# New slot tables for the last ticks with a scan, and another order of projections and loads in the first ones

## The reference

```python
k = rope(x @ Wk.T)                      # 16 heads of 32
v = x @ Wv.T
W = eye(32) per batch and head
for each block of 16 tokens:            # 256 blocks, strictly in order
    z = kc @ W
    W = W - kc.T @ ((z - vc) * 2 / (16 * 32))
out = layernorm(z over all heads) * gamma + beta
x1 = layernorm(x + out @ Wo.T)
h = silu(x1 @ gate.T * gs) * (x1 @ up.T * us)        # 1408 wide
y = layernorm(x1 + (h @ down.T) * ds)
```

## Time and profile before

| | |
|---|---|
| median of three runs | 1948.31 us |
| the profiled execution | 1948.8 us |
| its span | 1946.7 us |
| TensorE busy | 1856.2 us, 95% |
| VectorE, GpSimd, ScalarE busy | 61%, 33%, 28% |
| DMA | 288.29 MB, mean 148 GB/s |
| mean granted TensorE clock | 0.982 |

### The profile page before, as it was taken

How to read it: one execution, slowest core, us unless ns; L and a number is a source line. 1 busy time by engine, 2 the same in 40 slices (tenths; PEclk the granted TensorE clock), 3 DMA queues, 4 the chain that set the end, 5 groups by cost and what they waited for, 6 DMA issues and landing times.

```text
span 1946.7 us, 60662 instructions
## 1 busy us (share of the span) xinstructions
PE 1856.2 (95%) x25784; PEld 1482.0 (76%) x25784; DVE 1185.3 (61%) x2602; ACT 550.7 (28%) x1238; POOL 652.1 (33%) x783
## 2 busy tenths in 40 slices
PE   7868999999999999999999999999999999888897
PEld 5647787787778778877877777777777777767776
DVE  3655666666666566666666666666666665555543
ACT  3212323232222223222232223233322322222222
POOL 2222333333333333333333333333333333323333
PEclk9978999999999999999999999999999999999999
DMA  8974444554544554554455454445545544443310
GB/s 282 289 225 136 149 138 144 168 155 142 157 147 135 148 163 143 159 149 132 143 161 165 134 155 148 137 145 166 159 141 154 151 126 135 124 123 110 101 61 23
DMA packets 310783, 288.29 MB, mean 148 GB/s; under 512 B 43376, under 2 KB 261616, under 8 KB 310512
## 3 DMA queue, kind: packets, MB, share of 16 engines
q1 hardware_dynamic: 297840, 266.57, 45.9%
q10 hardware_dynamic: 12672, 17.83, 2.8%
HBM read 153.17 MB, written 139.72 MB: 150 GB/s over the span
## 4 chain that ended last, share of the span: by engine, by line
PE 80%; DVE 10%; DMA 4%; SPq 2%; ACT 2%; issue 1%; ACTq 0%; POOL 0%; POOLq 0%; DVEq 0%
PE gu_acc L973 32%; PE work L954 25%; PE down_acc L987 13%; PE scan_acc L926 4%; PE scan_acc L943 4%; DVE x_tok L1153 2%; DMA landed<-x1T_scr 2%; DVE state L1233 2%; DVE hid L1238 2%; DVE turned L1158 2%; SPq L327 1%; ACT hid L689 1%; PE scan_acc L973 1%; SPq L372 1%; PE down_acc L954 1%
## 5 line engine op out<-in xcount | busy, mean ns | idle before, releaser
L579 POOL TENSOR_TENSOR hid_lo<-hid,hid_hi 128x256 fp32r<-128x256 f32 x352 | 262.6, 746 | 644.3 <-ACT hid_hi L699 644.2
L973 PE MATMUL gu_acc<-x_hi,gw 128*128 128x256 f32 x1372 | 379.5, 309 | 11.4 <-DVE hid L1238 5.8
L689 ACT ACTIVATE hid<-gu_acc,gate_scale 128x256 f32<-128x256 f32 x343 | 162.7, 474 | 780.8 <-PE gu_acc L973 780.5
L1238 DVE SCALAR_TENSOR_TENSOR hid<-gu_acc,up_scale,hid 128x256 f32<-128x256 f32 x343 | 165.6, 483 | 317.6 <-ACT hid L689 317.4
L973 PE MATMUL gu_acc<-x_lo,gw 128*128 128x256 f32 x1372 | 343.5, 283 | 0.0
L973 PE MATMUL gu_acc<-x_hi,uw 128*128 128x256 f32 x1372 | 341.4, 281 | 0.0
L973 PE MATMUL gu_acc<-x_lo,uw 128*128 128x256 f32 x1372 | 340.4, 281 | 0.0
L1233 DVE SCALAR_TENSOR_TENSOR state<-scan_acc,half_step,state 128x256 f32<-128x256 f32 x512 | 223.3, 477 | 165.9 <-PE scan_acc L943 161.2
L973 PEld LDWEIGHTS gu_acc<-x_hi,gw 128*128 128x128 f32 x1372 | 261.1, 190 | 48.2 <-DVE hid L1238 21.8
L987 PE MATMUL down_acc<-dw,hid_hi 128*128 128x512 f32 x704 | 282.3, 401 | 2.3 <-POOL hid_lo L579 2.2
L987 PE MATMUL down_acc<-dw,hid_lo 128*128 128x512 f32 x704 | 279.1, 396 | 0.0
(11 more groups left out here) (129 smaller groups left out, 2251.6 us busy)
## 6 DMA issues: line engine op xcount, KB each, us to landing
x_fm<-xT SPq DMA_DIRECT2D x64, 256.0 KB, 3.5
k_rows<-k_scr SPq DMA_DIRECT2D x512, 32.0 KB, 2.0
z_scr<-v_rows SPq DMA_DIRECT2D x32, 512.0 KB, 3.2
z_tok<-z_scr SPq DMA_DIRECT2D x512, 32.0 KB, 1.8
x_tok<-x SPq DMA_DIRECT2D x32, 512.0 KB, 5.7
v_rows<-v_scr SPq DMA_DIRECT2D x496, 32.0 KB, 2.0
out<-x_tok SPq DMA_DIRECT2D x31, 512.0 KB, 2.8
kT_scr<-turned SPq DMA_DIRECT2D x120, 128.0 KB, 2.9
```

The lines of the kernel that those rows point to most:

```text
L579: pool.tensor_tensor(hid_lo[m % RING][:], hid[m % 2], hid_hi[m % RING][:].bitcast(F32), ALU.subtract).then_inc(hid_lo_ready, 1)
L689: act.activation(hid[m % 2], gu_bank(n, m)[:, 0:TOK], ACT.Silu, scale=gate_scale[:, m:m + 1]).then_inc(silu_done, 1)
L973: mm = pe.matmul(gu_bank(n, m)[:, k * TOK:(k + 1) * TOK], lhsT=w[:, c, m * P:(m + 1) * P].bitcast(dt), rhs=part[:, c].bitcast(dt), start=( ...
L1238: dve.scalar_tensor_tensor(hid[m % 2], gu_bank(n, m)[:, TOK:2 * TOK], up_scale[:, m:m + 1], hid[m % 2], ALU.mult, ALU.mult).then_inc(hid_r ...
```

## The change

There are three parts.

1. Ticks 29 to 32 count as late. Tick 29 (TURNING) and ticks 30 to 32 (LATE) get tables of their own, and tick 33 (WITHOUT_SCAN) takes the two blocks of its oldest tile that were done in the tick before. In late ticks all 11 blocks of a tile are in its own tick, 0 to 7 in slots 0 to 7 and 8 to 10 in slots 10 to 12; O is in slots 8 and 9; the z statistics are in slot 1, `turn_zn` in slot 3, the parts of z in slot 7, the norm of x1 in slot 11, `high_x1` and `low_x1` in slot 15.
2. ScalarE's queue loads x of tiles 3 to 6. SyncE's order in ticks 1 and 2 changes with it, and z of tile 0 is loaded in one go in tick 2. Six of the weight pieces are issued later, and all examinations but one or two move back.
3. K and V of tile 3 leave slots 12 to 15 of tick 1 and stand with K and V of tile 4 between slot 15 of tick 1 and tick 2.

```diff
-USUAL, WITHOUT_SCAN, END = None, NT + 1, NT + 2
+STEADY = 3
+LEAD = 3
+USUAL, TURNING, LATE, WITHOUT_SCAN, END = None, NT - LEAD, NT - LEAD + 1, NT + 1, NT + 2
 GATE_UP = {USUAL: {14: (2, 0), 15: (2, 1), 0: (3, 2), 2: (3, 3), 3: (3, 4), 5: (3, 5), 7: (3, 6), 8: (3, 7), 9: (3, 8),
                    10: (3, 9), 11: (3, 10)},
-           WITHOUT_SCAN: {0: (3, 2), 1: (3, 3), 2: (3, 4), 3: (3, 5), 4: (3, 6), 5: (3, 7), 6: (3, 8), 8: (3, 9),
-                          9: (3, 10), 11: (2, 0), 12: (2, 1), 13: (2, 2), 14: (2, 3), 15: (2, 4)},
+           TURNING: {0: (3, 2), 1: (3, 3), 2: (3, 4), 3: (3, 5), 4: (3, 6), 5: (3, 7), 6: (3, 8), 7: (3, 9), 10: (3, 10)},
+           LATE: {0: (3, 0), 1: (3, 1), 2: (3, 2), 3: (3, 3), 4: (3, 4), 5: (3, 5), 6: (3, 6), 7: (3, 7), 10: (3, 8),
+                  11: (3, 9), 12: (3, 10)},
+           WITHOUT_SCAN: {0: (3, 0), 1: (3, 1), 2: (3, 2), 3: (3, 3), 4: (3, 4), 5: (3, 5), 6: (3, 6), 7: (3, 7), 8: (3, 8),
+                          9: (3, 9), 10: (3, 10), 11: (2, 0), 12: (2, 1), 13: (2, 2), 14: (2, 3), 15: (2, 4)},
...
 DOWN = {USUAL: {15: (2, 0), 0: (3, 1), 2: (3, 2), 3: (3, 3), 5: (3, 4), 8: (3, 5), 9: (3, 6), 10: (3, 7), 11: (3, 8),
                 12: (3, 9), 13: (3, 10)},
+        TURNING: {0: (3, 1), 1: (3, 2), 2: (3, 3), 3: (3, 4), 4: (3, 5), 5: (3, 6), 6: (3, 7), 7: (3, 8), 8: (3, 9),
+                  11: (3, 10)},
+        LATE: {1: (3, 0), 2: (3, 1), 3: (3, 2), 4: (3, 3), 5: (3, 4), 6: (3, 5), 7: (3, 6), 8: (3, 7), 11: (3, 8),
+               12: (3, 9), 13: (3, 10)},
...
+       TURNING: DOWN[TURNING], LATE: DOWN[LATE], WITHOUT_SCAN: DOWN[WITHOUT_SCAN], END: DOWN[END]}
-WEIGHED = {(1, 5): (0,), (1, 8): (1,), (1, 11): (2,), (1, 13): (3,), (2, 0): (4,), (2, 2): (5,), (2, 4): (6,), (2, 6): (7,),
-           (2, 9): (8,), (2, 10): (9,), (2, 11): (10,), (2, 13): (11,)}
+WEIGHED = {(1, 6): (0,), (1, 10): (1,), (1, 13): (2,), (2, 0): (3,), (2, 2): (4,), (2, 4): (5,), (2, 6): (6,), (2, 9): (7,),
+           (2, 10): (8,), (2, 11): (9,), (2, 12): (10,), (2, 13): (11,)}
-FIRST_UNITS = ((K, 1, 1), (V, 1, 1), (K, 2, 0), (V, 2, 0), (K, 2, 1), (V, 2, 1), (K, 3, 0), (V, 3, 0))
-MIDDLE_UNITS = ((K, 3, 1), (V, 3, 1), (K, 4, 0), (V, 4, 0))
+FIRST_UNITS = ((K, 1, 1), (V, 1, 1), (K, 2, 0), (V, 2, 0), (K, 2, 1), (V, 2, 1))
+MIDDLE_UNITS = ((K, 3, 0), (V, 3, 0), (K, 3, 1), (V, 3, 1), (K, 4, 0), (V, 4, 0))
+def late(t):
+    return NT - LEAD <= t <= NT
```

On SyncE:

```diff
                     store_v(1, 1)
-                    load_x_fm(3)
+                    load_k_half0(1)
                     store_z(0, 0, NS // 2)
-                    load_k_half0(1)
-                    load_z(0, 0, NS // 2, 16)
                     store_v(2, 0)
+                    store_k(2)
+                    store_v(2, 1)
                     load_v_half0(1, 0)
                     load_v_half0(1, 1)
-                    store_k(2)
                     store_z(0, NS // 2, NS - 1)
-                    store_v(2, 1)
-                    load_x_fm(4)
-                    load_z(0, NS // 2, NS - 1, 32)
                     store_kT(2)
                     store_z(0, NS - 1, NS)
-                    load_z(0, NS - 1, NS, 48)
                 elif t == 2:
                     load_k_half1(1)
                     load_v_half1(1)
                     store_v(3, 0)
+                    load_z(0, 0, NS, 48)
                     store_k(3)
                     store_v(3, 1)
-                    load_x_fm(5)
...
                     load_kT(2)
-                    load_x_fm(6)
                     load_x(0)
```

On ScalarE (the copies and loads of weights besides):

```diff
+                    if t == 1 and s == 7:
+                        load_x_fm(3)
+                    if t == 1 and s == 11:
                         high_x(3, 0)
                     if t == 1 and s == 13:
                         high_x(3, 1)
                     if t == 1 and s == 15:
+                        load_x_fm(4)
                         copy_v(3, 0)
                         high_x(4, 0)
                         copy_v(3, 1)
                         high_x(4, 1)
+                        load_x_fm(5)
                     if t == 2 and s == 1:
                         high_x(5, 0)
+                    if t == 2 and s == 4:
+                        load_x_fm(6)
...
+                    if t == 1 and s in (0, 4, 8, 12):
+                        load_ffn(0, s // 4)
+                    if t == 1 and s in (2, 6, 10, 14):
+                        copy_ffn(1, s // 4)
+                    if t == 1 and s == 15:
                         load_ffn(1, 0)
+                        copy_ffn(2, 0)
+                    if t == 2 and s == 0:
                         load_ffn(1, 1)
                         copy_ffn(2, 1)
+                    if t == 2 and s == 1:
                         load_ffn(1, 2)
+                    if t == 2 and s == 2:
                         copy_ffn(2, 2)
+                    if t == 2 and s == 3:
                         load_ffn(1, 3)
+                    if t == 2 and s == 4:
                         copy_ffn(2, 3)
+                    if t == 2 and s in (5, 6, 7, 8):
+                        load_ffn(2, s - 5)
```

On TensorE (VectorE, ScalarE and GpSimd follow in the same way):

```diff
-                    if within(o) and s in (6, 7):
-                        project_o(o, s - 6)
+                    if within(o) and s in ((8, 9) if late(t) else (6, 7)):
+                        project_o(o, s % 2)
```

More of the change, by code:

```diff
@@ L67, in within @@
     return 0 <= n < NT
+def late(t):
+    return NT - LEAD <= t <= NT
 def unit_at(table, t, s):
-    age, m = table.get(t, table[USUAL]).get(s, (0, -1))
+    age, m = table.get(LATE if late(t) and t != TURNING else t, table[USUAL]).get(s, (0, -1))
     return (t - age, m) if m >= 0 and within(t - age) else None
@@ L627, in tick @@
                         copy_k_cols(t, 0)
-                    if within(o) and s == 9:
+                    if within(o) and s == (11 if late(t) else 9):
                         inverse_root(1, o)
@@ L631, in tick @@
                         low_hid(*unit_at(LOW, t, s))
-                    if within(o) and s == (3 if o == 0 else 4 if o == LAST else 1):
+                    if within(o) and s == (3 if o == 0 else 4 if o == LAST else 2 if late(t) else 1):
                         inverse_root(0, o)
@@ L637, in tick @@
                         add_rotated(n, 1)
-                    if within(o) and s == 4:
+                    if within(o) and s == (7 if late(t) else 4):
                         add_bias(o, 0)
@@ L802, in tick @@
                         high_hid(*unit_at(LOW, t, s))
-                    if within(o) and s == (6 if o == LAST else 5):
+                    if within(o) and s == (6 if o == LAST else 7 if late(t) else 5):
                         high_zn(o, 0)
@@ L812, in tick @@
                         save_z(sc, s // 2)
-                    if within(o) and s == (6 if o in (0, LAST) else 5):
+                    if within(o) and s == (6 if o in (0, LAST) else 7 if late(t) else 5):
                         high_zn(o, 1)
@@ L843, in tick @@
                         high_x(n + 1, 1)
-                    if within(o) and s == (12 if o != LAST else 10):
+                    if within(o) and s == (10 if o == LAST else 15 if late(t) else 12):
                         high_x1(o, 0)
@@ L1375, in tick @@
                         scale_hid(*unit_at(GATE_UP, t, s))
-                    if within(o) and s == (2 if o == 0 else 3 if o == LAST else 0):
+                    if within(o) and s == (2 if o == 0 else 3 if o == LAST else 1 if late(t) else 0):
                         dve.wait_ge(z_tok_in, 256 * (o + 1))
@@ L1386, in tick @@
                         normalize(2, yn, 1, y_tok, y_tok, y_ready)
[L1387 removed]
+                    if within(o) and s == (10 if late(t) else 8):
                         moments_of(1, o)
[L1389 removed]
+                    if within(o) and z_by_dma(o) and s == (11 if late(t) else 9):
                         turn_x1(o, 1)
```

86 lines of the change are left out of this document (29 added, 57 removed).

## The result

| | before | after |
|---|---|---|
| median | 1951.03 (1947.59 to 1955.94, 8 runs) | 1964.07 (1959.90 to 1971.55, 8 runs) |
| profiled execution, span | 1948.8, 1946.7 | 1960.76, 1958.6 |

What follows compares the result with a forecast made beforehand. TensorE was taken as busy except at the two ends, with late ticks set by a dependency loop. Front -10 and tail +13 made 1948.8 - 10 + 13 = 1951.8, stated as 1951, range 1937 to 1962.

Steps and rivals of the forecast that it cites:

- (a): Tick 1: K and V of tile 3 move behind slot 15, tick 2 starts at about 87.4, gain 1.6.
- (b): Start of tick 2 to slot 8: x of tile 5 issued earlier, 30.6 instead of 44.2, gain 13.6.
- (e): Tick 2: x_tok of tile 0 in at about 111, O0's sum asks at 113; next wait if DMA is late.
- (c): Tick 2, slots 9 to 14: one more reduce of 1.60 on VectorE, loss 1.6.
- The rival that the front's gain is lost: Front: x loads wait behind weight pieces on ScalarE's ring, gain 3 or less, result 1958 to 1962; chance 0.20.
- (h): Late ticks, x1 turned to gate 0: 11.6 less a state step of 0.88, so 10.7.
- (g): Late ticks, O0 to x1 turned: second O unit waits for the first's sum, 16.7 instead of 16.1.
- (f): Late ticks, gate 0 to O0: eight gates and downs first, plus a slow first gate, 28.4 instead of 26.4.
- Tick 32: Tail: no SyncE row loads between x1 store and load, tick of 54.4, gate 0 of tick 33 at 1872.7.
- Tick 33 and behind: End: two more gates and downs at 3.0, 1.9 for slow gate and hid wait, about 1.9 made up.
- tail keeps its length: Rival: tables only shift work, tail within 2 of before, 1938; chance 0.13.
- tail tightens: Rival: ticks 30 to 32 fall to 50 as O no longer waits for z, 1925; chance 0.07.

Runs made afterwards that it cites:

- the sum first: Changed kernel with VectorE's sum of the output projection ahead of the state step in slots 9 and 10 of late ticks: 1951.44, ratio 1.0003 to before.
- old-slots kernel: Changed kernel with late ticks' z stages, O and norm of x1 in their earlier slots, gates 6 to 10 in slots 7 to 11: 1950.55, ratio 1.0010 to before.
- filler: Changed kernel with added matmuls that nobody reads on TensorE in slots 14 and 15 of the late ticks: 1962.75, ratio 1.0055 to before.

## Why the prediction was wrong

The signs of both halves were right, and the front nearly so in size. Wrong was the size of the tail.

- **(a) Tick 1.** Predicted gain 1.6; from the start of tick 1 to that of tick 2 it was 1.4 (54.45, from 34.18 to 88.63, instead of 55.83). Right.
- **(b), (e) Tick 2 to slot 8.** Predicted 13.6, less 3.6 of DMA lateness. The wait of 10.31 went, and the transfers grew as worked out (14.75 MB, I had said 15.6). The wait that (e) named as next, the sum of O0 for x_tok, came, with 6.65 where I had 2.0. The O unit behind it took 4.59, where I had 3.0 though the earlier trace rows show 4.58 for it. The stretch took 37.7 instead of 44.2: gain 6.5. The shortfall was 7, twice what I took, and inside the range of 0 to 16.
- **(c) The extra reduce.** Predicted loss 1.6; slot 8 to tick 3 took 30.05 instead of 31.54, a gain of 1.5. The wait for the examined weights (3.76, 2.75 before) grew by 1.0, less than the reduce of 1.6. The largest part of what made the rest shorter is the clock: the second gate of the stretch took 2.0 instead of 3.6 (not shown).
- **Front in all:** tick 3 starts 8.3 earlier, 1.7 short of my 10. One us of this lies ahead of the change: tick 1 began at 34.18, 1.05 later than in the profile of before. The rival that the front's gain is lost falls by its price, but its mechanism isn't refuted: x of tile 5, issued with no piece ahead of it, landed in 3.7, while x of tiles 3, 4 and 6, each behind a piece, took 5.4, 7.8 and 7.8. TensorE waited for none of them longer than before.
- **Tick 29, (h).** Gate 0 of tick 30 was due at 1704.5, with the front's 8.1 off 1696.4; it came at 1696.73.
- **(g) O0 to x1 turned.** Predicted 16.7, measured 17.1. Right as a count, and yet the largest thing that I read past: 1.9 of it was a wait made by the order of two instructions, 7.8 over four ticks, and with the sum first the kernel is level with before (1.0003).
- **(f) Gate 0 to O0. The step that failed.** I took "1.2 since the first gate after a wait runs slow", from one row of before in which a single gate took 3.38, and gave one tick 0.8 for a second. Measured are two slow gates in three of four ticks: 30.4, 28.2, 30.4 where I had 28.4. The earlier trace rows followed a stretch in which gates and downs still kept TensorE busy. The new tables themselves empty the stretch ahead of gate 0, busy for 4.7 of 13.7 in tick 29, so the row came from a stretch that the change removes. Over ticks 30 to 33 seven gates were slow and cost 10.9 more than gates of 2.15; with the 1.08 that gate 1 of tick 33 waits for hid that is 12.0. My sum had 6.3 for it (three times 1.2, 0.8 and 1.9), so this term alone is 5.7 short.
- **Tick 32.** Predicted 54.4 since SyncE is free of row loads there, measured 57.42: 2.0 too little in (f), 0.4 in (g), and x1 took 10.0 and not 9.3 back from its turn to gate 0.
- **Tick 33 and behind.** Predicted +6.0 net: two gates and downs, 1.9 for the slow gate and the wait for hid, 1.9 given back. From gate 0 to the last down it is 83.1; before, from gate 2, 72.7: +10.4. Both gates ran slow, gate 1 waited 1.08 for hid, and on balance nothing was given back: the wait of 0.94 ahead of the second O unit went, but after the O units came new waits of 1.92 and 1.21, where waits of 0.31 and 0.46 for the low half stood before. The credit of 1.9 had no row under it.

The tail came to +20.0 where I had +13.3: 4.4 of the gap are tick 33 and behind, 3.0 tick 32, and ticks 29 to 31 are together 0.7 better than forecast, since the 56.5 that I took for a tick lay 0.7 above my own loop of 55.8 and tick 31 had one slow gate only. That part is luck: the signs that I had named for ticks 30 and 31 (56 to 57.5, a wait of about 1.7 ahead of the second O unit) all but came, and I had named none for tick 32 and what follows, where the gap lies. The end of my tail's range, +18 "with both first gates slow every tick", counted the clock as a thing at the edge. It was the rule. The rivals *tail keeps its length* and *tail tightens* fell as argued: O waits for TensorE's own order and not for transfers. (Gate 0 is another matter, as x1 comes back only just in time.) The old-slots kernel adds that even with O early the uncovered scan parts hold the tick at 54.9, close to the "about 54.4" that I gave as the lower end.

## What to carry to other kernels

When a table packs the covering work of a tick to its front, price the stretch that it leaves bare: every short dependent step there shows its whole round trip, and here the engine's clock fell (to 0.50), so that the first work behind it paid too, and not by the amount that the old schedule showed. When a unit moves to another slot, look at the order of its consumers on the other in-order engines at the new place: here the sum of an output projection stood behind a state step whose input TensorE makes only later, and putting it ahead took 1.96 us off each of four ticks. And move loads forward only as far as the DMA has room, since what was on time before may become the next wait. And before reading a wait as the work of an edit, look at it in another kernel that leaves that stretch alone: here such a pair differed by 1.6 us.

## What the runs showed of the hardware

- Two gates in a row of 3.7 to 3.8 instead of 2.1, at a granted clock of 0.50, after stretches in which TensorE was busy for 34% (13.7 us) and 46% (7.6 us). After a stretch with filler, busy for 65% of 8.6 us, both ran at 1.00, but after another of 61%, itself at 1.00, the two took 2.83 and 3.78. A stretch as sparse as the second, ahead of tick 31 (47%), was followed by one slow gate only (3.29). So the busy share alone doesn't tell which of the gates are slow; what does stays open.
- With the DMA full at 374 GB/s, the two v stores of 256 KB took 5.5 and 8.5 where the median had been 4.4, a load of 512 KB 7.0 instead of 4.5, and pieces of 704 KB 12.2. The x loads of 256 KB on the queue of those pieces landed in 3.7 with none ahead of them and in 5.4 to 7.8 behind one.
- The same front, in two kernels that differ only from tick 29 on, showed a wait of 6.44 and one of 4.84 ahead of the second O unit.
